# A Mamba, attention and MoE layer on one core: GpSimd makes three of the sixteen u*B products, and their decay moves into the PSUM ring

## The reference

```
xz = x @ W_in.T;  x_ssm, z = split(xz)
x_ssm = silu(conv(x_ssm) + conv_b)
proj = x_ssm @ W_x.T                 # B (16), C (16), one step value
dt = softplus(proj[..., -1:] * W_dt + b_dt);  A = -exp(A_log)
h = exp(dt * A) * h + (x_ssm * dt) * B      # per channel and state index, over time
y = sum_n h * C + x_ssm * D
x = layernorm(x + (y * silu(z)) @ W_out.T)
```

## Time and profile before

| | us |
|---|---|
| median of 3 runs | 1684.76 (1684.32 to 1684.80) |
| the profiled execution, its own time | 1675.18 |
| its span | 1673.4 |
| mean granted TensorE clock | 0.919 of full speed |

### The profile page before, as it was taken

How to read it: one execution, slowest core, us unless ns; L and a number is a source line. 1 busy time by engine, 2 the same in 40 slices (tenths; PEclk the granted TensorE clock), 3 DMA queues, 4 the chain that set the end, 5 groups by cost and what they waited for, 6 DMA issues and landing times. The chain is left out here.

```text
span 1673.4 us, 22601 instructions
## 1 busy us (share of the span) xinstructions
PE 1335.8 (80%) x7484; PEld 930.7 (56%) x7484; DVE 1465.3 (88%) x2698; ACT 1114.0 (67%) x2452; POOL 915.1 (55%) x663
## 2 busy tenths in 40 slices
PE   7687778788777877787886969988988898887880
PEld 5566556666656666565665644446445644462460
DVE  5999999999999999999999966697869786978578
ACT  5867887788788778878877524337633763375570
POOL 1778878877887788788778701102710271027015
PEclk9889899989989898998898989999999999999895
DMA  7201210220122022102102012100010000000000
GB/s 234 67 14 45 70 58 13 70 70 32 40 70 71 1 70 70 50 21 70 64 1 89 14 38 103 36 1 1 26 55 1 1 26 26 1 1 1 25 1 25
DMA packets 37927, 69.87 MB, mean 42 GB/s; under 512 B 3569, under 2 KB 31570, under 8 KB 33586
## 3 DMA queue, kind: packets, MB, share of 16 engines
q1 hardware_dynamic: 37810, 68.43, 12.0%
HBM read 59.77 MB, written 8.65 MB: 41 GB/s over the span
## 5 line engine op out<-in xcount | busy, mean ns | idle before, releaser
L900 POOL TENSOR_TENSOR state_c<-state,c_area 128x1024 f32<-128x1024 f32 x256 | 602.0, 2362 | 167.8 <-DVE state L970 148.9
L970 DVE TENSOR_TENSOR_SCAN state<-decay,ps 128x512 f32<-128x512 f32 x512 | 620.6, 1212 | 0.0
L686 ACT ACTIVATE decay<-step_area,negA 128x255 f32<-128x255 f32 x1024 | 432.6, 496 | 0.4 <-DVE step_area L1049 0.4
L945 DVE TENSOR_TENSOR ps<-step_area,ps 128x512 f32<-128x512 f32 x512 | 349.7, 683 | 8.0 <-PE ps L368 6.2
L384 PE MATMUL ps<-ident_sb,state_c 128*128 128x128 f32 x2048 | 293.3, 291 | 12.9 <-POOL state_c L900 11.9
L1578 POOL TENSOR_TENSOR big<-big,g_sb 128x1024 f32<-128x1024 f32 x29 | 79.4, 2739 | 406.6 <-ACT big L1467 404.9
L384 PEld LDWEIGHTS ps<-ident_sb,state_c 128*128 128x128 f32 x2048 | 253.5, 151 | 39.0 <-POOL state_c L900 21.5
L368 PE MATMUL ps<-parts,sel_bc_sb 96*128 96x256 bf16 x256 | 74.7, 292 | 102.7 <-DVE ps L961 80.2
L1391 PE MATMUL ps<-w_sb,weights 128*128 128x512 f32 x256 | 122.6, 615 | 0.0
L1426 PE MATMUL ps<-w_sb,hT 128*128 128x256 f32 x512 | 120.0, 388 | 2.4 <-ACT hT L1536 1.9
L1666 DVE BATCH_NORM_STATS2 stats<-big 128x6 f32<-128x256 f32 x256 | 88.4, 413 | 30.4 <-ACT big L1541 21.1
(11 more groups left out here) (211 smaller groups left out, 2357.9 us busy)
## 6 DMA issues: line engine op xcount, KB each, us to landing
c_area<-c_scratch SPq DMA_DIRECT2D x32, 1024.0 KB, 6.5
weights<-in_xT SPq DMA_DIRECT2D x16, 256.0 KB, 3.1
res<-in_x SPq DMA_DIRECT2D x16, 256.0 KB, 2.8
x_scratch<-res SPq DMA_DIRECT2D x16, 256.0 KB, 8.1
weights<-x_scratch SPq DMA_DIRECT2D x4, 1024.0 KB, 8.1
xa<-x_scratch SPq DMA_DIRECT2D x4, 1024.0 KB, 5.6
out_x<-acc SPq DMA_DIRECT2D x4, 1024.0 KB, 4.4
w_sb<-in_w SPq DMA_DIRECT2D x2, 1024.0 KB, 13.0
```

Source lines behind the costliest of these rows:

```text
L686: nc.scalar.activation(decay[:, n % RING, j, 1:], dt_sb[:, i[1] % 2, j, 1:], ACT.Exp, scale=negA[:, j * NS + n:j * NS + n + 1]).then_inc(s ...
L900: nc.gpsimd.tensor_tensor(state_c[:, n % RING, :, :], state[:, n % RING, :, :], c_bc[:, q, n, :].unsqueeze(1).to_broadcast([P, CT, TC]), A ...
L945: nc.vector.tensor_tensor(bu_ps[m % 3][:, :].rearrange("p (j n) -> p j n", j=2), u_sb[:, i[1] % 2, 2 * h:2 * h + 2, :], b_ps[n % 2][:, 0:T ...
L970: nc.vector.tensor_tensor_scan(state[:, n % RING, pair, :].rearrange("p j n -> p (j n)"), decay[:, n % RING, pair, :].rearrange("p j n -> ...
```

## The change

Three of the 16 state indices, n = 3, 6 and 9 (`OFF`), are made another way:

- GpSimd makes their u*B for all 4 channel groups in one instruction (`product_b`) into SBUF (`ub`, two tiles), and adds the carry itself. Its B rows come as fp32 through DRAM, in one more broadcast load per chunk (384 KB); `b_row`, `make_bu` and `add_carry` skip these n.
- Their decay goes into the PSUM banks that bu had: `psum_decay` on ScalarE, called after the decay of step n + 1, writes each half when the third user of banks ahead of it has been scanned, and clears the first token's column with a small copy. The scan reads decay from PSUM and bu from SBUF.
- The other 13 keep their way. The order in the lists changes: `silus` stands at step 9 (it was 10), `take_z(k, 1)` stays at 9; TensorE's `y_back` at 10 and 11 (11 and 12), `out_tile` at 12 and 13 (13 and 14), ScalarE's `take_y_back` at 13 and 14 (14 and 15), one `take_sum` at 15 of the same turn, `normalise` at 13 (9), `spreads` at 5 (3), `guess` at 8 (6).
- GpSimd's small norm instructions lose two of nine by fusing, `centre` stands at step 14 of the turn before.
- The two expert weight loads (2 MB) move from the start of the program to the start of `attn_ffn_block`.

```
+        OFF, APART = (3, 6, 9), 3
...
+        def bu_free(i, n, h):
+            p = USERS.index((n, h))
+            return scanned(i if p >= 3 else shift(i, -1), *USERS[p - 3])
...
             def load_c(k):
...
+                rows = bc_dram[bass.ds(at(k, BC, OFF[0]), APART * NO), :].rearrange("(a s) n -> a s n", s=APART)
+                sp.dma_start(b_bc[:, :, :], rows[:, 0, :].partition_broadcast(P)).then_inc(s_bb, 16)
...
             def b_row(i, n):
+                if n in OFF:
+                    return
...
                 if finish:
-                    early_by = 0 if prepare else 1
-                    work += [(11 - early_by, lambda: y_back(last, 0)), (12 - early_by, lambda: y_back(last, 1)),
-                             (13 - early_by, lambda: out_tile(last, 0)), (14 - early_by, lambda: out_tile(last, 1))]
+                    work += [(10, lambda: y_back(last, 0)), (11, lambda: y_back(last, 1)),
+                             (12, lambda: out_tile(last, 0)), (13, lambda: out_tile(last, 1))]
...
             def step(i, n):
...
+                if n in KEPT:
+                    for j in range(CT):
+                        nc.scalar.activation(decay_tile(i, n)[:, j, 1:], dt_sb[:, i[1] % 2, j, 1:], ACT.Exp,
+                                             scale=negA[:, j * NS + n:j * NS + n + 1]).then_inc(s_decay, 1)
+                if n - 1 in OFF:
+                    psum_decay(i, n - 1)
+
+            def psum_decay(i, n):
+
+                for h in range(2):
+                    act.wait_ge(s_scan, bu_free(i, n, h))
+                    bank = bu_bank(i, n, h)[:, :].rearrange("p (j n) -> p j n", j=2)
+                    nc.scalar.activation(bank[:, :, 0], zeros[:, :], ACT.Copy)
+                    for e in range(2):
+                        j = 2 * h + e
+                        nc.scalar.activation(bank[:, e, 1:], dt_sb[:, i[1] % 2, j, 1:], ACT.Exp,
+                                             scale=negA[:, j * NS + n:j * NS + n + 1]).then_inc(s_decay, 1)
...
-                    work += [(0, lambda: take_sum(old, 0)), (1, lambda: take_sum(old, 1)), (3, lambda: spreads(old)), (6, lambda: guess(old)),
-                             (9, lambda: normalise(old))]
+                    work += [(0, lambda: take_sum(old, 1)), (5, lambda: spreads(old)), (8, lambda: guess(old)),
+                             (13, lambda: normalise(old))]
...
+            def product_b(i, n):
+
+                c, later = OFF.index(n), i[1] % CPB
+                if c == 0:
+                    pool.wait_ge(s_u, at(i, 1, 1))
+                    pool.wait_ge(s_bb, at(i, 16, 16))
+                if c >= 2:
+                    pool.wait_ge(s_scan, scanned(i, OFF[c - 2], 1))
+                elif not is_first(i):
+                    pool.wait_ge(s_scan, scanned(shift(i, -1), OFF[c - 2], 1))
+                tile = ub_tile(i, n)
+                nc.gpsimd.tensor_tensor(tile, u_sb[:, i[1] % 2, :, :], b_bc[:, c, :].unsqueeze(1).to_broadcast([P, CT, TC]),
+                                        ALU.mult).then_inc(s_ub, 1 if later else 2)
...
+                work += [(2, lambda: product_b(i, OFF[1])), (5, lambda: product_b(i, OFF[2]))]
+                if prepare:
+                    work.append((15, lambda: product_b(k, OFF[0])))
...
             def scans(i, n, h):
...
+                if n in OFF:
+                    if h == 0:
+                        dve.wait_ge(s_ub, at(i, 2 * NO, 2 * OFF.index(n) + 2))
+                    a, b = bu_bank(i, n, h)[:, :], flat(ub_tile(i, n))
+                else:
+                    dve.wait_ge(s_bu, at(i, 4 * NK, 8 + 4 * rank(n) + 2 * h + 2))
+                    a, b = flat(decay_tile(i, n)), bu_bank(i, n, h)[:, :]
+                dve.wait_ge(s_decay, at(i, NS * CT, EMIT.index(n) * CT + 2 * h + 2))
...
-        LOADS = 4
+        LOADS = 6
```

More of the change, by code:

```diff
@@ L43, with mamba_block @@
 TG = 4
-def mamba_block(nc, x, xT, w_in, w_x, w_out, par, ident_sb, ident, sel_bc, sel_p, c_dram, x1, ahead, s_ahead, ps, early, late, shared,
+def mamba_block(nc, x, xT, w_in, w_x, w_out, par, ident_sb, ident, sel_bc, sel_p, bc_dram, x1, ahead, s_ahead, ps, early, late, shared,
                 w, ctxT):
@@ L64, in mamba_block @@
         SKIP_AT = 8
+        OFF, APART = (3, 6, 9), 3
+        KEPT = [n for n in range(NS) if n not in OFF]
+        NO, NK = len(OFF), len(KEPT)
+        USERS = [(n, h) for n in range(NS) for h in range(2)]
+        EMIT = []
+        for n in range(NS):
+            if n in KEPT:
+                EMIT.append(n)
+            if n - 1 in OFF:
+                EMIT.append(n - 1)
         w_ssm, diag_w, xi, w_gate, xT_sb, w_x_sb = (early[n] for n in ("w_ssm", "diag_w", "xi", "w_gate", "xT", "w_x"))
@@ L148, in mamba_block @@
         s_bu = sem("s_bu")
+        s_ub = sem("s_ub")
+        s_bb = sem("s_bb")
         s_scan = sem("s_scan")
@@ L186, in shift, with rank, scanned, bu_bank @@
             return (i[0], i[1] + n)
+        def rank(n):
+            return sum(m < n for m in KEPT)
+        def scanned(i, n, h):
+            return at(i, 2 * NS, 2 * RING + 2 * n + h + 1)
+        def bu_bank(i, n, h):
+            return bu_ps[at(i, len(USERS), USERS.index((n, h))) % 3]
+        def bu_free(i, n, h):
+            p = USERS.index((n, h))
+            return scanned(i if p >= 3 else shift(i, -1), *USERS[p - 3])
+        def decay_tile(i, n):
+            return decay[:, at(i, NK, rank(n)) % RING, :, :]
+        def ub_tile(i, n):
+            return ub[:, at(i, NO, OFF.index(n)) % 2, :, :]
         def is_first(i):
@@ L792, in _ @@
             turns(act, turn)
-            for t in range(CTT):
-                take_sum(shift(last, -1), t)
+            take_sum(shift(last, -1), 1)
             take_query(G + 1)
@@ L905, in turn @@
                             what()
+            nc.gpsimd.memset(zeros[:, :], 0.0)
             nc.gpsimd.memset(decay[:, :, :, 0], 0.0).then_inc(s_zero, 1)
[L908 to L910 removed]
             pool.sem_inc(s_sum, RING)
@@ L917, in _ @@
             injections(first, 0, NS - RING)
+            product_b(first, OFF[0])
             turns(pool, turn)
@@ L920, in _ @@
             for k in (shift(last, -1), last):
[L921 removed]
+                if k == last:
+                    centre(k)
                 variance(k)
@@ L1063, in _, with attn_ffn_block @@
             round_neg(1)
-def attn_ffn_block(nc, x1, ctxT, ident_sb, w, ps, late, shared, bo, g2, be2, bias_rows, before, out):
+def attn_ffn_block(nc, x1, ctxT, ident_sb, w, w1, w2, ps, late, shared, bo, g2, be2, bias_rows, before, out):
     U = G * NL
@@ L1931, in decoder_block @@
             ahead.append((w[name][tuple(slice(None) for _ in shape)], source))
-        mamba_block(nc, x, xT, w_in, w_x, w_out, par, ident_sb, ident, sel_bc, sel_p, c_dram, x1, ahead, s_ahead, ps, early, late,
+        mamba_block(nc, x, xT, w_in, w_x, w_out, par, ident_sb, ident, sel_bc, sel_p, bc_dram, x1, ahead, s_ahead, ps, early, late,
                     shared, w, ctxT)
-        attn_ffn_block(nc, x1, ctxT, ident_sb, w, ps, late, shared, bo, g2, be2, bias_rows, before, out)
+        attn_ffn_block(nc, x1, ctxT, ident_sb, w, channels(w1), channels(w2), ps, late, shared, bo, g2, be2, bias_rows, before, out)
 def _constants():
```

120 lines of the change are left out of this document (63 added, 57 removed).

## The result

The changed kernel takes **1697.28 us** (median of 4 runs, 1695.27 to 1701.77), the kernel before 1684.54 beside it (1682.09 to 1684.8): ratio 1.0083, 95% interval 1.006 to 1.0105. It is 12.7 us slower, where the forecast was 1693 in a range of 1668 to 1712 and slower by more than 0.2% had the chance 0.57. The two traces therefore differ by 26.6 us and the medians by 12.7; the other 13.9 are spread between executions. The size of a change I take from the ratio. The waits, and how they add up, I take from the traces.

The account below looks back on a forecast made before the run. VectorE's instruction stream was taken to bound the 927 us recurrence. The terms -56.2 + 58.6 + 6 = +8.4 us gave 1683.6 on the profiled execution; with the median standing 9.6 above it, 1693 us, range 1668 to 1712.

Parts of the forecast that it names:

- VectorE's gain: Recurrence on VectorE: six bu products fewer per chunk and fewer carry additions, net 3.5 to 3.6 us a chunk, -56 us.
- ScalarE's chain: ScalarE from decay 6 through z and Silus to decay 9: 15.6 us against VectorE's 11.9, +58.6 us in all.
- TensorE's order: TensorE's y_back and out_tile ahead of B's row 15 at the chunk's edge: 0.4 us a chunk, +6 us.
- the terms listed for its 14.2 us: ScalarE's work from the scan of n = 9 to its copy that y_back of tile 1 awaits, 14.2 us.
- the longer wait brings the low clock: TensorE's output tile: low clock followed 2.3 us waits, now 3.4, so B's row 15 is late by 0 or 1.5 us.
- The last chunk has no Silus and keeps its gain: Last chunk of the recurrence: no Silus on ScalarE, so no loss priced there and VectorE's saving stays.
- The sum: Whole kernel: -56.2 + 58.6 + 6 = +8.4 us on the profiled execution's 1675.2, giving 1683.6.
- The first two terms: Recurrence: VectorE's saving of -56.2 us and ScalarE's added wait of +58.6 us.
- The weight loads: Expert weight loads moved to the later stage's start: hidden before VectorE first waits for constants, otherwise some us, once.
- GpSimd, nothing: GpSimd's added products and additions: 52.7 us of work a chunk, under VectorE's 54.4, so they cost nothing.
- VectorE stays the bound: Rival for the recurrence: ScalarE needs 11.9 us or less between decays, time 1629; chance 0.08.
- its cases in between: Rival's cases where half the z waits on ScalarE and TensorE vanish, 2.3 us a chunk or part: 1655 to 1680; chance 0.17.

Follow-up runs that it names:

- e11: e10 with GpSimd's make_dt, first decay argument, second split, make_u and injections one step later, behind a state*C product; 1660.03 us, ratio 0.9882 to the kernel before.
- e4: The change with one more unused Silu of 128x1024 on ScalarE in each preparation; 1720.03 us, ratio 1.0246 to the kernel before.
- e12: e11 with state indices 3, 6, 9 in place of 2, 5, 8, nothing else different; 1683.26 us, ratio 0.9995 to the kernel before.
- e6: The change with only TensorE's y_back and out_tile back at steps 11 to 14; 1698.66 us, ratio 1.0097 to the kernel before.
- e7: The change with TensorE's attention values and queries one step later in the last chunk; 1690.59 us, ratio 1.0053 to the kernel before.
- e9: The kernel before, all 16 products on VectorE and decays in SBUF, with only the change's moved steps; 1697.85 us, ratio 1.0081.
- e8: The change with one more unused 128x1024 product on GpSimd at step 7 of each chunk but the last; 1697.55 us, ratio 1.0095.
- e10: The change with indices 2, 5, 8, e7's last chunk, ScalarE's copies and y take-backs earlier, normalise later, GpSimd's first product earlier; 1695.01 us, ratio 1.0066.
- e1: The change with ScalarE's Silus back at step 10, behind the PSUM decay of n = 9; 1729.21 us, ratio 1.0294 to the kernel before.
- e2: The change with state indices 2, 5, 8 in place of 3, 6, 9; 1701.14 us, ratio 1.0122 to the kernel before.
- e5: e2 with TensorE's y_back and out_tile one place later, at steps 11 to 14; 1708.97 us, ratio 1.0171 to the kernel before.

## Why the prediction was right, and where it was not

- **VectorE's gain, -56:** 58.5 in after and 54.4 in e11, each worked out from the last scan's time and the waits. The scan with swapped operands takes 1208 ns, 1210 the others.
- **ScalarE's chain, 3.7 us at n = 9 in 15 chunks, +58.6:** measured 3.75 to 5.08, the first 5.99, 63.3 in all, and 0.9 for the other scans. e4 (load on it) and e12 against e11 (other indices, the orders the same) show it as the cause of that idle. z's second tile waits 2.01 us as worked out.
- **TensorE's order, +6:** B-row waits grew by 19.9. The last chunk holds 16.8 of the 27.9 (13.37, 1.39, 1.36 and 0.67; 2.7 before). The other 15 chunks went from 5.3 to 11.1 us, 0.4 more each. The size per chunk was right, and so was the wait of 3.4 us for y's first tile (3.37 in most chunks), although the terms listed for its 14.2 us add up to 14.35. What I feared from it did not come: behind the 3.37 us y's second tile ran at full clock, 0.66 us in 12 of 13 chunks, where behind the 2.3 us of the kernel before it took 1.12 in most. The output tiles' products took 403 ns each in after and 456 before. So the reading that the longer wait brings the low clock was wrong.
- **"The last chunk has no Silus and keeps its gain": this step failed.** I listed what it does not have and not what it has: attention's context copies on ScalarE behind the new PSUM decay, and its values on TensorE ahead of B's row 7. B-row waits in that chunk grew by 14.1 us, more than the forecast's whole +8.4. Some 6 us of it is the low clock that lasted through the values in this execution (13.37 us against 7.01 in e6); the rest is the order, of which e7 gives part back. In e9, without the PSUM decay and with ScalarE's lists in the last chunk as in the change, the two waits there are 0.95 and 0.93.
- **The sum.** The terms came to +8.4 on the profiled execution, 1683.6. In the traces they are -58.5 + 64.2 + 19.9 = +25.6, and the profiled execution took 1701.8: 18 us beyond the sum, most of it the last chunk. The first two terms nearly cancel, as forecast. The medians moved by 12.7 only, because the traced execution of before was faster than its median and that of after slower than its own. That the forecast of 1693 lies within 4 us of 1697 is in part luck: how much of the last chunk's 14 us is in the other executions is not known. The direction and the mechanism of the two large terms are not luck.
- **What the sum did not hold.** The moved steps cost as much without any PSUM decay (e9), in other chunks and by other waits. I priced them only inside the new kernel, where 0.4 us a chunk was right. With the waits for B rows of the other chunks gone, indices 3, 6, 9 come to nothing (e12, 0.9995).
- **The weight loads, some us at most:** from the last scan to the end of the span it took 716.3 us before, 717.4 in after, and 717.6 in e9, which leaves the loads where they were. They cost nothing that shows.
- **GpSimd, nothing:** right for this change (e8), wrong as a general statement: with the chain gone it held take_y for 33.8 us (e10).
- **The rival "VectorE stays the bound", 1629 to 1680:** it did not happen. e11 comes to its cases in between only after TensorE's, ScalarE's and GpSimd's orders were changed too, and my expectations for e1, e2 and e5 (1650 to 1670) repeated the error of that rival: they took away one wait and asked nothing about the next.
- **The product on GpSimd:** 2360 ns, 2362 before, so unchanged beside VectorE. The rule of the Trainium skill (GPSIMD Engine Reference, Engine selection) gives elementwise products to VectorE and calls GpSimd about half as fast with two inputs. The trace agrees on the ratio, 2360 ns against 1.22 us. e11 shows that with VectorE the full engine it can still pay to go against the rule.

## What to carry to other kernels

When the fullest engine is relieved, list for each in-order queue what stands just ahead of what that engine needs, and price every one of these waits before calling the first the bound: here a wait of 1 to 4 us a chunk on another queue took the place of each one removed (e1, e2, e5, e10). Look at the stages that differ from the steady one (the last chunk) for what they have, not for what they lack. And an instruction moved to an earlier place costs what it waits for: a wait on GpSimd that one product can be moved ahead of was worth 1.8% here (e11 against e10).

## What the runs showed of the hardware

- An Exp of 128x255 with a scale from a tile takes 458 ns into PSUM and 496 into SBUF, but in a row the slot is 0.40 us for both (two into PSUM are busy 0.86, four into SBUF 1.69).
- TensorE's granted clock fell to 0.50 (1.2 GHz) within some of its waits for ScalarE: at 905.2 in a wait of 3.82 us in the kernel before, at 922.7 in one of 3.95 in after, at 654.5 in one of 3.42 in e2, where the work behind took 3.62 us in place of 1.95. It did not fall in every one: behind the 3.42 us at 243.25 in e2 the row product took 0.70 us and not 1.22, and behind the 3.37 us ahead of y's second tile in after the clock was 1.00. In that chunk of e2 it fell only at 244.7, when TensorE was at work again.
- How long the low level then lasted differs as much: 7 us in the kernel before, 30 in after, 10 in e6, for the same place in the program. It set how long attention's values took, 3.75 us or 1.95, and with that how long VectorE waited for the B row behind them.
